# Adding u to the destination rows on GpSimd instead of VectorE, with u in two buffers

## The chip, the cores and the metric

The kernel runs on one core of a Trainium2 chip. The metric is the device time of one execution in microseconds; the time before is the median of three runs. Engines are named as the profile names them: PE is TensorE's matmul side and PEld its weight loads, DVE is VectorE, ACT is ScalarE, POOL is GpSimd, SP is SyncE, which here only issues DMAs.

## The reference, cut to what matters

The network is four graph layers over 100,000 nodes with 64 features and 50,000 edges sorted by destination. The change touches the end of the first layer, graph attention with four heads: per edge the source row `hs` and the destination's own row `hd` are each weighted by head, added, projected by `gatw`, summed over the edges of one destination, biased and passed through a leaky relu of slope 0.01. The result is added to the node's row x.

```python
    alpha = ex / denom[d2]
    o = jax.ops.segment_sum(xh[s2] * alpha[:, :, None], d2, num_segments=n)
    o = jnp.mean(o, axis=1) + gat_b
    return _leaky(o, NEG_ACT)
...
    x = x + _L0_gnn_ref(h, edge_index, edge_weight, ...)
```

## The kernel before

The edges are cut into 49 groups of 1024 (128 partitions by S = 8 slots, C = 64 features each). The program is a row of stages with a barrier between them; every engine has its own loop over the groups in each stage. The stage in question is `attention_sums`. `ring_loop` gives each engine, in step s, the work of group s minus a lag, in the order of the numbers that the generators yield; four steps are unrolled in a hardware loop. Engines meet only at semaphores, and each engine works strictly in its written order.

In step s the engines do the following.

- DVE: copies a count of group s-1 (L1902, short "copy"), multiplies the source rows by the weights into `at_wide` for s-1 (L1903, "mul"), scans the projected sums of s-3 (L1308, "scan"), forms u = max(slant, row) of s-4 from PSUM and `at_slant` (L1922, "u"), adds u to the destination rows `at_xd` into `at_x1` (L1928, "x"; the profile calls the tile `at_x`), and adds the own rows to the last six slots of `at_wide` of s-1 (L1908, "add").
- POOL: multiplies the own rows of slots 0 to 3 of group s (L1880, "own"), then, once DVE's mul of s is done, adds the first two slots into `at_wide` (L1883, "joined").
- PE: transposes the weights of s (L1938), transposes `at_wide` of s-2 (L1950), transposes the biased sums of s-4 back (L412), and multiplies by `gatw` for s-2 (L1959), which waits for the scan of the group before.
- ACT: evacuates the weights (L1977) and the transposed rows (L1993, "pf"), computes `at_slant` (L2007, "slant"), the biased sums (L2000), and 16 small products of the own rows (L1984).
- SP: issues the loads of the groups, the load of `at_xd` four groups ahead, and the store of `at_x1`; the last two wait for the semaphore `x1_done`.

What a step counts from in this text is the start of its scan, called S.

Of the kernel before, what the change touches and what calls it, by code (L numbers as in the profile page):

```python
# [22 lines left out]
ALU = mybir.AluOpType  # L23
# [8 lines left out]
P = 128  # L32
C = 64
S = 8
# [3 lines left out]
GROUPS = -(-EDGES // G_ROWS)  # L38
# [19 lines left out]
RING = 4  # L58
# [24 lines left out]
def take_turns(stages):  # L83

    due = [(0, k, gen) for k, gen in enumerate(stages)]
    while due:
        due.sort(key=lambda x: x[:2])
        t, k, gen = due.pop(0)
        nxt = next(gen, None)
        if nxt is not None:  # L90
            assert nxt >= t, (nxt, t)
            due.append((nxt, k, gen))


def ring_loop(eng, n, *lags, lead=0, ring=RING):

    k_max = max(len(lags) + 1, lead)
    assert n > k_max + ring

    def step(group_of):  # L100
        started = []
        for k, stages in enumerate(lags):
            at = group_of(k)
            if at is not None:
                started += [s for s in (f(*at) for f in stages) if s is not None]
        take_turns(started)

    def fixed(s):
        def at(k):
            g = s - k  # L110
            return (g // ring, g % ring, g) if 0 <= g < n else None
        step(at)

    for s in range(k_max):
        fixed(s)
    turns = (n - k_max) // ring
    with eng.Fori(0, turns) as i:  # L117
        for q in range(ring):
            def at(k):
                off = k_max + q - k  # L120
                return i + off // ring, off % ring, i * ring + off
            step(at)
    for s in range(k_max + ring * turns, n + len(lags) - 1):
        fixed(s)


def hold(eng, sem, value):


    if not (isinstance(value, int) and value < 1):  # L130
        eng.wait_ge(sem, value)  # L131
        eng.sem_inc(HELD[0], 1)  # L132


def after(eng, sem, value):

    if not (isinstance(value, int) and value < 1):
        eng.wait_ge(sem, value)
# [6 lines left out]
def half_turns(i, r):  # L145

    return i * 2 + r // 2
# [295 lines left out]
def as_rows(x):  # L443
    return x.rearrange("p (s c) -> p s c", c=C)
# [14 lines left out]
def build(nc, A, out):  # L459
    ctx = ExitStack()  # L460
    with ctx:
# [101 lines left out]
        with ExitStack() as kept:  # L563
# [7 lines left out]
            phase(attention_sources, W, D, bank, M)  # L571
            phase(attention_weights, W, D, bank, M)
        phase(attention_sums, W, D, bank)
        phase(gated_messages, W, D, bank)
        phase(relu_messages, W, D, bank, out)
# [1251 lines left out]
def attention_sums(nc, A, sem, W, D, bank):  # L1827

    ctx = ExitStack()
    with ctx:  # L1830
        t = lambda n, sh, dt=F32: ctx.enter_context(nc.sbuf_tensor(n, sh, dt))
        col = W.col
        hs, hd = (t("at_" + n, [P, 2, S, C]) for n in ("hs", "hd"))
        xd, x1 = t("at_xd", [P, RING, S, C + 1]), t("at_x1", [P, 2, S, C])
# [3 lines left out]
        pf = t("at_pf", [P, 2, 2, HALF])  # L1838
        sums = t("at_sums", [C, 2, G_ROWS])
        biased = t("at_biased", [C, 2, G_ROWS])  # L1840
        slant, u = (t("at_" + n, [P, S, C]) for n in ("slant", "u"))
        names = ("al_t", "al_done", "wide_step", "joined", "own_done", "own_rest", "wide_t", "pf_done", "mm", "carry", "biased_done", "u_done",
                 "back", "slanted", "x1_done")
        m = {n: sem("at_" + n) for n in names}
        inn, st = ([sem(f"at_{n}{k}") for k in (0, 1)] for n in ("in", "st"))
        x_in = [sem(f"at_x_in{r}") for r in range(RING)]
        with nc.Block() as block:
            @block.sync
            def _(sp):
                for k in (0, 1):  # L1850
                    sp.sem_inc(st[k], 16)

                def load(i, r, g):
                    hold(sp, m["wide_step"], g * 2 + 1)
                    sp.wait_ge(m["own_done"], g + 1)
                    sp.wait_ge(m["own_rest"], g + 1)
                    for b, d in ((hs, D.hs), (hd, D.hd)):
                        sp.dma_start(b[:, r % 2], group_rows(d)[g]).then_inc(inn[r % 2], 16)
                    sp.dma_start(alpha[:, r % 2], group_cols(D.alpha)[g]).then_inc(inn[r % 2], 16)

                def load_x(i, r, g):
                    sp.wait_ge(m["x1_done"], g + 1)
                    sp.dma_start(xd[:, r], group_rows(D.xd)[g]).then_inc(x_in[r], 16)

                def store(i, r, g):
                    sp.wait_ge(m["x1_done"], g + RING + 1)
                    sp.dma_start(group_rows(D.x1d)[g], x1[:, r % 2]).then_inc(st[r % 2], 16)
                ring_loop(sp, GROUPS, [load], [], [load_x], [], [], [], [store])
                for k in (0, 1):
                    sp.wait_ge(st[k], ODD_EVEN[k] + 16)  # L1870

            @block.gpsimd
            def _(pool):
                def own_rows(i, r, g):
                    hold(pool, inn[r % 2], half_turns(i, r) * 48 + 48)
                    hold(pool, m["al_done"], g + 1)
                    hold(pool, m["wide_step"], g * 2 + 2)
                    rows = hd[:, r % 2, 0:S // 2].unsqueeze(2).to_broadcast([P, S // 2, HEADS, C])
                    by = al[:, r % 2, 0:S // 2, HEADS:2 * HEADS].unsqueeze(3).to_broadcast([P, S // 2, HEADS, C])
                    nc.gpsimd.tensor_tensor(own[:, r % 2, 0:S // 2], rows, by, ALU.mult).then_inc(m["own_done"], 1)  # L1880
                    hold(pool, m["own_done"], g + 3)
                    hold(pool, m["wide_step"], g * 2 + 5)
                    nc.gpsimd.tensor_tensor(wide[:, r % 2, 0:JOINED], wide[:, r % 2, 0:JOINED], own[:, r % 2, 0:JOINED], ALU.add  # L1883
                                            ).then_inc(m["joined"], 1)
                ring_loop(pool, GROUPS, [own_rows])

            @block.vector
            def _(dve):
                dve.sem_inc(m["wide_step"], 4)
                dve.sem_inc(m["own_done"], 2)  # L1890
                dve.sem_inc(m["own_rest"], 2)
                dve.sem_inc(m["x1_done"], RING)
                nc.vector.memset(sums[:, 1, G_ROWS - 1:G_ROWS], 0.0).then_inc(m["carry"], 1)

                def a(i, r, g):
                    yield 1
                    dve.wait_ge(inn[r % 2], half_turns(i, r) * 48 + 48)
                    dve.wait_ge(m["al_done"], g + 1)
                    after(dve, m["wide_t"], g * 2 - 2)
                    by = hs[:, r % 2].unsqueeze(2).to_broadcast([P, S, HEADS, C])  # L1900
                    wt = al[:, r % 2, :, 0:HEADS].unsqueeze(3).to_broadcast([P, S, HEADS, C])
                    nc.vector.tensor_copy(W.countE[:, bass.ds(g, 1)], al[:, r % 2, :, 2 * HEADS].unsqueeze(1))  # L1902
                    nc.vector.tensor_tensor(wide[:, r % 2], by, wt, ALU.mult).then_inc(m["wide_step"], 1)  # L1903
                    yield 4
                    dve.wait_ge(m["wide_step"], g * 2 + 5)
                    dve.wait_ge(m["own_done"], g + 3)
                    dve.wait_ge(m["own_rest"], g + 3)
                    nc.vector.tensor_tensor(wide[:, r % 2, JOINED:S], wide[:, r % 2, JOINED:S], own[:, r % 2, JOINED:S], ALU.add  # L1908
                                            ).then_inc(m["wide_step"], 1)

                def scan(i, r, g):
                    yield 2
                    dve.wait_ge(m["mm"], g + 1)
                    dve.wait_ge(m["carry"], g + 1)
                    after(dve, m["biased_done"], g - 1)
                    run_sums(nc, W, g, r % 2, bank(4, 2)[0:C], sums, m)

                def x(i, r, g):
                    yield 3
                    dve.wait_ge(m["slanted"], g + 1)  # L1920
                    after(dve, m["x1_done"], g + RING)
                    nc.vector.scalar_tensor_tensor(out=u[:], in0=as_rows(bank(1)), scalar=0.0, in1=slant[:], op0=ALU.add,  # L1922
                                                   op1=ALU.max).then_inc(m["u_done"], 1)
                    yield 3
                    dve.wait_ge(x_in[r], i * 16 + 16)
                    dve.wait_ge(st[r % 2], half_turns(i, r) * 16 + 16)
                    dve.wait_ge(m["u_done"], g + 1)
                    nc.vector.tensor_tensor(x1[:, r % 2], xd[:, r, :, 0:C], u[:], ALU.add).then_inc(m["x1_done"], 1)  # L1928
                ring_loop(dve, GROUPS, [], [a], [], [scan], [x])

            @block.tensor
            def _(pe):
# [658 lines left out]
```

## Time and profile before

| what | value |
|---|---|
| median of three runs | 5640.13 us (5633.73 to 5650.66) |
| profiled execution, its span from the first instruction to the last | 5641.0 us |
| busy in the span: PE, DVE, ACT, POOL | 66%, 74%, 42%, 67% |
| mean granted PE clock | 0.777 |
| the stage `attention_sums` | 2963 us to 3371 us |

The page gives the profiled execution by its span alone. The shares of the whole span are averages over stages with different limits. The stage of the change is 408 us of the 5641, so it is read by itself.

### The profile page before, as it was taken

What the parts mean: (1) busy time and instruction counts of PE and PEld (TensorE: products, weight loads), DVE (VectorE), ACT (ScalarE), POOL (GpSimd) and SP (SyncE); (2) the same over time, 40 slices, a digit from 0 to 9 for tenths busy, and PEclk for the clock granted to TensorE, in tenths of its full rate; (3) what the DMA queues carried; (4) which work ended last, traced back from release to release, by engine and by line L of the source; (5) the groups of instructions that cost most, each with busy time, mean ns of one, the idle gap of its engine ahead of it and who ended that gap; (6) DMA issues with size and microseconds to landing.
All of it is one profiled execution on the core that took longest, in us unless ns stands there. A gap on an engine that the chain in (4) does not pass through costs nothing. (4 is left out here: it accounts for less than half of the span.)

```text
span 5641.0 us, 69641 instructions
## 1 busy us (share of the span) xinstructions
PE 3732.6 (66%) x15267; PEld 1851.4 (33%) x15267; DVE 4168.8 (74%) x6266; ACT 2361.1 (42%) x4957; POOL 3788.1 (67%) x3734
## 2 busy tenths in 40 slices
PE   8997788847776999677727876777555546552110
PEld 3443555533332333244414442333222212221000
DVE  8876789957774555788868988999655559996442
ACT  0000678833331222466618973343222247772221
POOL 7776766767775777577724337666377767774777
PEclk9998899977876555788869998899766568885555
DMA  5533987744442222455524433333244423332221
GB/s 59 77 53 56 153 203 226 234 136 107 107 106 55 61 63 61 141 182 171 181 64 129 137 117 76 82 83 82 79 130 131 131 69 76 76 73 65 68 72 51
DMA packets 538641, 595.34 MB, mean 106 GB/s; under 512 B 300576, under 2 KB 315046, under 8 KB 536923
## 3 DMA queue, kind: packets, MB, share of 16 engines
q1 hardware_dynamic: 319004, 473.91, 28.7%
q0 software_dynamic: 115712, 91.82, 9.1%
q10 hardware_dynamic: 103840, 28.71, 4.2%
q14 instruction: 59, 0.48, 0.0%
q8 instruction: 26, 0.43, 0.0%
HBM read 354.69 MB, written 303.31 MB: 117 GB/s over the span
## 5 line engine op out<-in xcount | busy, mean ns | idle before, releaser
L1135 POOL DMA_INDIRECT l_got<-d_x,l_near x1176 | 1157.6, 984 | 557.5 <-issue 354.6
L1135 POOL DMA_INDIRECT p_got<-d_h,p_near x392 | 440.2, 1123 | 155.8 <-issue 118.9
L848 PE MATMUL ps<-hot_lo,hot_w 128*128 128x512 bf16 x2352 | 510.0, 380 | 13.4 <-DVE hot_lo L785 13.4
L1135 POOL DMA_INDIRECT p_got<-d_sums,p_near x392 | 401.4, 1024 | 151.7 <-issue 149.3
L2457 POOL DMA_INDIRECT out<-fi_res,fi_near x392 | 381.0, 972 | 181.1 <-issue 118.2
L726 POOL DMA_INDIRECT d_pos<-place,near x392 | 400.2, 1021 | 125.2 <-issue 119.1
L1135 POOL DMA_INDIRECT p_got<-d_ext,p_near x392 | 382.2, 975 | 132.4 <-issue 117.1
L1143 POOL DMA_INDIRECT ln_xd<-d_xt,idsE x304 | 286.9, 944 | 136.8 <-issue 96.9
L2131 PE MATMUL ps<-l_hid,w2n 128*64 128x512 f32 x392 | 234.8, 756 | 162.2 <-DVE l_sums L1308 155.7
L412 PE MATMUL ps<-ident,fi_sums 64*128 64x64 f32 x392 | 53.1, 314 | 424.8 <-DVE fi_sums L1308 424.8
L848 PEld LDWEIGHTS ps<-hot_lo,hot_w 128*128 128x128 bf16 x2352 | 230.6, 98 | 293.2 <-issue 17.3
L782 DVE SCALAR_TENSOR_TENSOR hot_w<-iota_hi,hiS,vals 128x384 bf16<-128x384 bf16 x392 | 241.1, 615 | 80.8 <-PE ps L848 78.2
L1308 DVE TENSOR_TENSOR_SCAN p_sums<-same,p_sums,ps 65x1024 f32<-65x1024 f32 (+1 forms) x98 | 229.6, 2343 | 93.5 <-PE ps L1407 89.5
L405 PE MATMUL ps<-ident,l_hn 128*128 128x128 f32 x588 | 112.2, 323 | 221.4 <-DVE l_hn L2236 196.9
L419 PE MATMUL ps<-l_df,l3ab 128*64 128x512 f32 x196 | 164.8, 995 | 127.5 <-DVE l_neg L2357 127.5
L1308 DVE TENSOR_TENSOR_SCAN l_sums<-same,l_sums,ps 64x1024 f32<-64x1024 f32 (+1 forms) x98 | 228.7, 2334 | 0.4
L1883 POOL TENSOR_TENSOR at_wide<-at_wide,at_own 128x512 f32<-128x512 f32 x49 | 70.3, 1434 | 215.9 <-DVE at_wide L1903 214.7
L1959 PE MATMUL ps<-at_pf,gatw 128*64 128x512 f32 x392 | 178.3, 598 | 54.1 <-DVE at_sums L1308 53.5
L2524 DVE TENSOR_TENSOR fi_res<-fi_xd,ps 128x512 f32<-128x512 f32 x49 | 33.5, 684 | 241.7 <-POOLq L2464 241.7
L419 PE MATMUL ps<-l_hf,l2w 128*64 128x512 f32 x196 | 176.8, 1058 | 46.5 <-ACT l_hf L2280 46.5
L863 ACT ACTIVATE near<-finE 128x8 int32 (+1 forms) x49 | 10.2, 208 | 467.3 <-DMA d_pos<-place,near 467.3
L2545 ACT ACTIVATE ps<-fi_hh,fi_sc 64x1024 f32<-64x1024 f32 x49 | 59.0, 1205 | 337.0 <-DMA fi_hh<-d_hh 333.1
(391 smaller groups left out, 10871.3 us busy)
## 6 DMA issues: line engine op xcount, KB each, us to landing
l_xd<-d_x SPq DMA_DIRECT2D x147, 256.0 KB
d_ext<-ln_ext SPq DMA_DIRECT2D x98, 264.0 KB
d_xt<-in_x_wide ACTq DMA_DIRECT2D x49, 520.0 KB
ln_x<-in_x SPq DMA_DIRECT2D x98, 256.0 KB
d_h<-ln_hb SPq DMA_DIRECT2D x98, 256.0 KB, 2.9
d_x<-ln_x SPq DMA_DIRECT2D x98, 256.0 KB
lb_x<-d_x SPq DMA_DIRECT2D x49, 512.0 KB
d_x<-lb_x SPq DMA_DIRECT2D x49, 512.0 KB
```

Of the source, the lines that this page charges most:

```text
L405: last = nc.tensor.transpose(out[:, P * n:P * n + P], flat[:, P * n:P * n + P], W.ident[:])
L419: last = nc.tensor.matmul(out[:, HALF * h:HALF * h + HALF], weights[:, h], paired, start=True, stop=True)
L726: nc.gpsimd.indirect_dma_start(out=D.pos, out_offset=bass.IndirectOffsetOnAxis(ap=near[:, r, q:q + 1], axis=0), in_=at[:, r, q:q + 1], in_ ...
L782: nc.vector.scalar_tensor_tensor(out=hot_w[:, r], in0=wide(iota_hi[:], PARTS), scalar=hs[:, one], in1=vt.unsqueeze(2).to_broadcast([P, PAR ...
L848: last = nc.tensor.matmul(bank(h), hot_w[:, r, k], hot_lo[:, r, 512 * h:512 * h + 512], start=False, stop=False)
L1135: nc.gpsimd.indirect_dma_start(out=out[:, q], out_offset=None, in_=source, in_offset=bass.IndirectOffsetOnAxis(ap=ids[:, q:q + 1], axis=0) ...
L1143: nc.gpsimd.indirect_dma_start(out=out[:, q], out_offset=None, in_=source, in_offset=bass.IndirectOffsetOnAxis(ap=ids[:, g, q:q + 1], axis ...
L1308: return nc.vector.tensor_tensor_scan(sums[:, par], same, messages, sums[:, 1 - par, G_ROWS - 1:G_ROWS], ALU.mult, ALU.add).then_inc(m["ca ...
L1883: nc.gpsimd.tensor_tensor(wide[:, r % 2, 0:JOINED], wide[:, r % 2, 0:JOINED], own[:, r % 2, 0:JOINED], ALU.add).then_inc(m["joined"], 1)
L1959: last = nc.tensor.matmul(bank(4, 2)[0:C, HALF * h:HALF * h + HALF], W.gatw[:, q], pf[:, h, q], start=q == 0, stop=q == 1)
L2131: last = nc.tensor.matmul(msg[:, part], W.w2n[:], hid[k][:, part], start=k == 0, stop=k == 1)
L2457: nc.gpsimd.indirect_dma_start(out=out, out_offset=bass.IndirectOffsetOnAxis(ap=near[:, r, q:q + 1], axis=0), in_=res[:, r, q], in_offset= ...
```

## The change

x is taken from DVE's list and put into POOL's, at the same lag of four groups. In POOL's code the lag decides only the group; within a step POOL runs own, joined, x in that order. `at_u` becomes two buffers, so u of a group may be written while x of the group before is still to come: DVE's u waits for the x of two groups before (`g + RING - 1`) instead of one. POOL's x waits for `at_xd`, for the store that used the same half of `at_x1`, and for u; `hold` is a wait followed by a semaphore increment.

```diff
-        slant, u = (t("at_" + n, [P, S, C]) for n in ("slant", "u"))
+        slant, u = t("at_slant", [P, S, C]), t("at_u", [P, 2, S, C])
...
-                ring_loop(pool, GROUPS, [own_rows])
+
+                def x(i, r, g):
+                    hold(pool, x_in[r], i * 16 + 16)
+                    hold(pool, st[r % 2], half_turns(i, r) * 16 + 16)
+                    hold(pool, m["u_done"], g + 1)
+                    nc.gpsimd.tensor_tensor(x1[:, r % 2], xd[:, r, :, 0:C], u[:, r % 2], ALU.add).then_inc(m["x1_done"], 1)
+                ring_loop(pool, GROUPS, [own_rows], [], [], [], [x])
...
-                def x(i, r, g):
+                def rows(i, r, g):
                     yield 3
                     dve.wait_ge(m["slanted"], g + 1)
-                    after(dve, m["x1_done"], g + RING)
-                    nc.vector.scalar_tensor_tensor(out=u[:], in0=as_rows(bank(1)), scalar=0.0, in1=slant[:], op0=ALU.add,
+                    after(dve, m["x1_done"], g + RING - 1)
+                    nc.vector.scalar_tensor_tensor(out=u[:, r % 2], in0=as_rows(bank(1)), scalar=0.0, in1=slant[:], op0=ALU.add,
                                                    op1=ALU.max).then_inc(m["u_done"], 1)
-                    yield 3
-                    dve.wait_ge(x_in[r], i * 16 + 16)
-                    dve.wait_ge(st[r % 2], half_turns(i, r) * 16 + 16)
-                    dve.wait_ge(m["u_done"], g + 1)
-                    nc.vector.tensor_tensor(x1[:, r % 2], xd[:, r, :, 0:C], u[:], ALU.add).then_inc(m["x1_done"], 1)
-                ring_loop(dve, GROUPS, [], [a], [], [scan], [x])
+                ring_loop(dve, GROUPS, [], [a], [], [scan], [rows])
```

On DVE, one step in the loop of the stage stood like this before (a scan is listed as SCALAR_TENSOR_TENSOR; ISA and REGISTER_ALU rows are waits and their register arithmetic).

```order
L1308 SCALAR_TENSOR_TENSOR at_sums<-same,at_sums,ps 64x1024
L1922 SCALAR_TENSOR_TENSOR at_u<-ps,at_slant 128x512
L1928 TENSOR_TENSOR at_x<-at_xd,at_u 128x512
L1905 REGISTER_ALU
L1906 REGISTER_ALU
L1908 TENSOR_TENSOR at_wide<-at_wide,at_own 128x1536
```

In the changed kernel the same step reads as follows; x is gone, and the add stands right behind u.

```order
L1308 SCALAR_TENSOR_TENSOR at_sums<-same,at_sums,ps 64x1024
L1928 SCALAR_TENSOR_TENSOR at_u<-ps,at_slant 128x512
L1911 REGISTER_ALU
L1912 REGISTER_ALU
L1914 TENSOR_TENSOR at_wide<-at_wide,at_own 128x1536
```

On POOL, this is a piece of the same loop before.

```order
L1880 TENSOR_TENSOR at_own<-at_hd,at_al 128x1024
L131 REGISTER_ALU x2
L1883 TENSOR_TENSOR at_wide<-at_wide,at_own 128x512
L131 REGISTER_ALU
L131 ISA
L1880 TENSOR_TENSOR at_own<-at_hd,at_al 128x1024
```

In the changed kernel x stands between joined and the next group's own.

```order
L1880 TENSOR_TENSOR at_own<-at_hd,at_al 128x1024
L131 REGISTER_ALU x2
L1883 TENSOR_TENSOR at_wide<-at_wide,at_own 128x512
L131 ISA x2
L131 REGISTER_ALU
L1890 TENSOR_TENSOR at_x<-at_xd,at_u 128x512
L131 REGISTER_ALU
L131 ISA
L1880 TENSOR_TENSOR at_own<-at_hd,at_al 128x1024
```

So x moved past every DVE instruction of a step and behind POOL's joined, and own of the next group now starts behind it. The order on PE, ACT and SP is the same as before.

## Rows read from the trace of the kernel before

**Rows 1.** Window of the steady part: busy us of each engine, PE clock.

```profile
core 0: us, PE busy (x) PEld busy (x) DVE busy (x) ACT busy (x) POOL busy (x), PEclk, DMA share, GB/s
...
3003.50:3351.60 348.10, 296.29 (x1754) 170.49 (x1752) 334.15 (x266) 326.34 (x924) 138.00 (x88) 1.00 0.47 138
```

**Rows 2.** Timeline of DVE, steady: start us, us, work, idle before and its releaser.

```profile
3153.85 2.33 DVE L1308 TENSOR_TENSOR_SCAN at_sums<-same,at_sums,ps 64x1024 f32<-64x1024 f32 x1
3156.28 0.69 DVE L1922 SCALAR_TENSOR_TENSOR at_u<-ps,at_slant 128x512 f32<-128x512 f32 x1
3157.08 0.72 DVE L1928 TENSOR_TENSOR at_x<-at_xd,at_u 128x512 f32<-128x512 f32 x1
3157.72 1.75 DVE L1908 TENSOR_TENSOR at_wide<-at_wide,at_own 128x1536 f32<-128x1536 f32 x1
3159.39 0.16 DVE L1902 COPY countE<-at_al 128x8 f32 x1
3159.47 2.28 DVE L1903 TENSOR_TENSOR at_wide<-at_hs,at_al 128x2048 f32<-128x2048 f32 x1
3161.67 2.33 DVE L1308 TENSOR_TENSOR_SCAN at_sums<-same,at_sums,ps 64x1024 f32<-64x1024 f32 x1
3164.30 0.69 DVE L1922 SCALAR_TENSOR_TENSOR at_u<-ps,at_slant 128x512 f32<-128x512 f32 x1 [0.30 <-ACT at_slant L2007]
```

**Rows 3.** Timeline of POOL, the same stretch.

```profile
3154.11 1.27 POOL L1883 TENSOR_TENSOR at_wide<-at_wide,at_own 128x512 f32<-128x512 f32 x1 [4.88 <-DVE at_wide L1903]
3155.35 1.90 POOL L1880 TENSOR_TENSOR at_own<-at_hd,at_al 128x1024 f32<-128x1024 f32 x1
```

**Rows 4.** Timeline of PE, the same stretch.

```profile
3156.57 3.62 PE L1959 MATMUL ps<-at_pf,gatw 128*64 128x512 f32 x8 [1.27 <-DVE at_sums L1308]
...
3160.71 1.97 PE L1950 MATMUL ps<-ident,at_wide 128*128 128x128 f32 x16
```

**Rows 5.** Timeline of ACT, the same stretch.

```profile
3163.67 0.60 ACT L2007 ACTIVATE at_slant<-ps 128x512 f32<-128x512 f32 x1
```

**Rows 6.** Timeline of DVE, the stage's head.

```profile
2973.12 1.76 DVE L1908 TENSOR_TENSOR at_wide<-at_wide,at_own 128x1536 f32<-128x1536 f32 x1 [1.86 <-POOL at_own L1880]
2974.79 1.23 DVE L1902 COPY countE<-at_al 128x8 f32<-128x8 f32 x1
2975.94 2.28 DVE L1903 TENSOR_TENSOR at_wide<-at_hs,at_al 128x2048 f32<-128x2048 f32 x1
```

**Rows 7.** Timeline of POOL, the stage's head.

```profile
2973.30 2.70 POOL L1883 TENSOR_TENSOR at_wide<-at_wide,at_own 128x512 f32<-128x512 f32 x1 [0.27 <-POOL at_own L1880]
2975.96 4.03 POOL L1880 TENSOR_TENSOR at_own<-at_hd,at_al 128x1024 f32<-128x1024 f32 x1
```

**Rows 8.** Timeline of DVE, the first steady step.

```profile
3003.55 2.33 DVE L1308 TENSOR_TENSOR_SCAN at_sums<-same,at_sums,ps 64x1024 f32<-64x1024 uint8 x1
...
3006.59 0.89 DVE L1928 TENSOR_TENSOR at_x<-at_xd,at_u 128x512 f32<-128x512 f32 x1
```

**Rows 9.** Timeline of POOL, the same step.

```profile
3005.03 1.90 POOL L1880 TENSOR_TENSOR at_own<-at_hd,at_al 128x1024 f32<-128x1024 f32 x1
```

**Rows 10.** Timeline of DVE, the last steady step's scan.

```profile
3351.58 2.33 DVE L1308 TENSOR_TENSOR_SCAN at_sums<-same,at_sums,ps 64x1024 f32<-64x1024 uint8 x1
```

**Rows 11.** Tile at_x on DVE: duration min/median/max in ns, first and last start.

```profile
L1928 DVE TENSOR_TENSOR at_x<-at_xd,at_u x49: 692/693/1173, 2998.5 to 3370.3; 128x512 f32<-128x512 f32 x49
```

**Rows 12.** Timeline of DVE, later in the head.

```profile
2986.40 2.34 DVE L1308 TENSOR_TENSOR_SCAN at_sums<-same,at_sums,ps 64x1024 f32<-64x1024 uint8 x1 [1.21 <-PE ps L1959]
2988.66 1.72 DVE L1908 TENSOR_TENSOR at_wide<-at_wide,at_own 128x1536 f32<-128x1536 f32 x1
...
2990.39 2.28 DVE L1903 TENSOR_TENSOR at_wide<-at_hs,at_al 128x2048 f32<-128x2048 f32 x1
```

**Rows 13.** Timeline of POOL, the same stretch as rows 12.

```profile
2987.29 6.50 POOL L1883 TENSOR_TENSOR at_wide<-at_wide,at_own 128x512 f32<-128x512 f32 x1 [0.34 <-POOL at_own L1880]
```

**Rows 14.** Window of the next stage, columns as in rows 1.

```profile
3500.00:3600.00 100.00, 74.40 (x287) 34.90 (x288) 96.88 (x171) 37.97 (x74) 69.92 (x68) 0.90 0.32 83
```

## The prediction

> **What bounds the kernel now.** I read the windows first, to find out which engine is full in the stage of the change. In the steady part, 348 us long, DVE is busy 96% of the time, ACT 94%, PE 85%, POOL 40%, and PE has its full granted clock (1.00, so 2.4 GHz) [rows 1]. The first scan of it starts at 3003.55 [rows 8], the last at 3351.58 [rows 10], 44 steps later: 7.91 us a step. These 44 steps are what the change can act on; the head of the stage (40 us) and its tail (19 us) are fills and drains.
>
> Then the timelines of one step. On DVE the starts follow each other by: scan to u 2.43 us, u to x 0.80, x to add 0.64, add to copy 1.67, copy to mul 0.08, mul to scan 2.20 [rows 2]. The sum is 7.82 us. Every second step or so u starts some tenths late behind ACT's slant (0.30 us idle at 3164.30 [rows 2]), which makes the mean 7.91. So DVE is the bound, but a second loop is nearly as long: from the end of a scan (3156.18) PE multiplies (3.62 us), then transposes the weights and `at_wide` [rows 4], ACT evacuates and forms slant, which ends at 3164.27 [rows 5], 8.09 us after the scan's end. The u that waits for it leads to the scan after next. Two steps along this loop are 8.09 + 0.03 + 0.80 + 0.64 + 1.67 + 0.08 + 2.20 + 2.33 = 15.84, that is 7.92 a step. Both loops contain x.
>
> The third thing to see is POOL. joined starts 0.26 us after the scan's start, own follows 1.24 us later and takes 1.90, so POOL is done at S+3.40 and then idles until the next mul is done, 4.88 us at joined's row [rows 3]. By busy share it has much room. But look at when it works: only while DVE runs scan and u.
>
> **DVE and POOL get in each other's way.** This is the row reading on which the forecast rests. In the head, own started when mul had just started and took 4.03 us instead of 1.90: it ends at 2979.99, which is 1.77 us after the mul's end at 2978.22 [rows 6, 7]. joined, started inside an add, took 2.70 instead of 1.27 and ended 1.12 after the add's end [rows 6, 7]. The copy behind that add took 1.23 us instead of 0.16 and ended with joined [rows 6, 7]. And x itself took 0.89 us when own was still running, against a median of 0.69 [rows 11]: own ended at 3006.93, x at 3007.48, so x really began 0.14 us before own's end [rows 8, 9]. In the steady step its 0.72 fits the same rule (own ends at 3157.25). Scan and u, which read one operand from PSUM, run beside POOL at full speed, and so does POOL: 2.33 and 0.69, 1.27 and 1.90 [rows 2, 3]. So in this trace a DVE instruction with both operands in SBUF (mul, add, x) and a POOL instruction never overlap: one waits to the end of the other, less 0.14 us of start-up.
>
> The Trainium skill says the same in "SBUF — State Buffer", section Who interferes with whom: DVE instructions with two SBUF inputs and GpSimd instructions that read SBUF share one port pair, and whoever issues first holds it for the whole instruction. The trace agrees where own took 4.03 us beside a mul; by the page's first-come order the step would be the 8.45 us worked out below, and there is one place in the trace where that order did not hold (rival B).
>
> **The change, part by part.** (1) x leaves DVE: u to add becomes 0.65 in place of 0.80 + 0.64 (the 0.80 holds a semaphore wait on u, the 0.64 is what an instruction of this size takes with none). DVE's own work is then 7.82 - 0.80 = 7.02 a step.
>
> (2) x on POOL. The trace has no x there; the nearest row is joined, the same 128x512 f32 addition, 1.27 us, followed by the next instruction after 1.24 [rows 3]. Lower bound: DVE's 0.69. Upper: 1.90, own with twice the elements. I take 1.27. x's three holds (each a wait and an increment) are processed while joined runs, and all are met: u was finished a step earlier, `at_xd` four groups ahead. The store two groups back has about two steps, some 16 us, against one and a half before, when x never waited for it.
>
> (3) Where x lands. joined S+0.26, x S+1.50, own S+2.74 to S+4.64. DVE has u at S+2.43 and wants the add, with both operands in SBUF, at S+3.08. own has started 0.34 us before that, so the add waits until 4.64 - 0.14 = S+4.50. From there add, copy and mul take 1.67 + 0.08 + 2.20, and the next scan starts at S+8.45. Before, own ended at S+3.40, just as x wanted to start at S+3.23: POOL's 3.14 us filled exactly the 3 us in which DVE leaves it alone. The change puts 1.24 us more into a window that was full and takes only 0.80 from DVE.
>
> (4) Does anything hide this? Queued behind x on POOL is own, for whose result the add of the next step waits, one step later: no wait. PE starts transposing `at_wide` at S+6.86 (3160.71 [rows 4]); the late add ends at 4.50 + 1.75 = S+6.25, in time. slant ends 2.33 + 8.09 = S+10.42, at a step of 8.45 that is 1.97 into the next, ahead of u at 2.43. So neither PE nor ACT adds to it nor covers it; the scan waits for DVE alone. SP's load of `at_xd` and the store wait for x, now later by nearly a step; both had more than that.
>
> (5) The second buffer of u costs nothing; with one, u would have waited for the x before, done at S+2.77, past u's S+2.43.
>
> (6) Ends of the stage: in the head the longest x (1.17 us [rows 11], half of it waiting for own) no longer stands before an add that would wait for the same own: about -0.6. The last x of the stage runs 1.27 for 0.69 on POOL: +0.6. They cancel.
>
> Sum: 44 x (8.45 - 7.91) = +23.8 us. On the profiled execution's 5641.0 that is 5664.8; this execution is 0.9 above the median of the runs, so I forecast 5664 for the median, 0.4% slower.
>
> **Rivals.** (A) *No collision that matters, and faster.* If the add took the port before own and own lost nothing by it, or POOL's additions read from elsewhere, the step would be the longer of 7.02 and the PE and ACT loop without x: (15.84 - 0.80) / 2 = 7.52. 44 x 0.39 = -17, 5623. It decides where own no longer stands between u and add. Against it stand four rows of collisions and no row of an overlap. 5%.
>
> (B) *Milder: POOL's work is packed tighter.* In one place joined was issued at 2987.29 during a scan with an add queued behind, and did not run: it ended at 2993.79, 1.12 after the end of the mul that began at 2990.39, having let add, copy and mul pass [rows 12, 13]. So a queued DVE instruction can be served first. If this happens behind u, own slips past the mul and POOL's three run in one piece from there: 1.12 for the one already waiting, then 1.24 and 1.90, with small overlaps 4.18 after S, giving a step of 4.18 + 3.95 = 8.13, 44 x 0.22 = +10, 5650. This is the least that exclusive use allows. But a group that is late on POOL makes PE wait for joined, and then PE's loop lengthens the step again toward 8.5. 15%, of which most is within 0.3%.
>
> (C) *Worse: own slips in behind the add*, as joined did in the head [rows 6, 7]. Then the add runs from S+3.08 to 4.83, own to 6.60, and the copy starts at 6.46, mul at 6.54, the scan at 8.74: 44 x 0.83 = +36, 5676. 10%.
>
> (D) *The clock.* PE's busy share falls from 85% to 6.73 / 8.45 = 80%. In the next stage PE is 74% busy and has a clock of 0.90 [rows 14], that is, part of it at 1.2 GHz. Were PE's work from its matmuls to the first half of the `at_wide` transposes (4.14 us between their starts, and 1.0 [rows 4]) to take twice as long, the loop without x would be (15.04 + 5.1) / 2 = 10.1 a step. If a tenth of the steady part fell to it: 4.4 x 1.7 = +7 on top, 5671. 10%.
>
> **How the numbers follow.** The forecast has 60%; its own range is 5658 to 5669, from x at 1.1 us (a step of 8.30) to 1.4 (8.58), with 44 steps each. Adding (B), (C) and (D) gives 5645 to 5678, which leaves out (A), and the rest of the surprises. What a measurement here tells from no change is about 0.3%, 17 us. Slower by more: nearly all of the forecast, (C) and (D), 0.77. Within: most of (B) and the low edge, 0.18. Faster: 0.05.
>
> **What would show it.** Right: in the changed profile the steady scans start 8.4 to 8.5 us apart; the add has a mean near 3.2 us (it waits inside its duration, as x's 0.89 did) in place of 1.75; x on POOL lasts 1.27 and starts 1.5 behind the scan; own starts at S+2.74 undisturbed at 1.90; slant no longer holds up u; DVE still looks 95% busy, by waiting. (B) would show as own or x of 5 to 6 us and adds at 1.75. (C) as a copy of 1.8 us. (A) as idle time of DVE before u behind slant and a step of 7.5. Wrong altogether would be a step below 7.9 or a stage that grew anywhere but in its steady part.

## The result, and the profile after

The changed kernel takes 5663.9 us (median of 6 runs, 5654.75 to 5666.86), beside 5639.69 us for the kernel before (6 runs, 5633.73 to 5650.66). The ratio is 1.0038, 95% interval 1.0026 to 1.0049: 15 to 28 us slower. The profiled execution of it took 5664.0 us, with a span of 5661.4; the span of the one before is 5641.0, so by spans it is +20.4. One run of the kernel before, on the second chip of the experiments, took 8855.53 us and is left out of the ratios.

The page's busy line, to be read against the one of before in the table above:

```profile
PE 3736.0 (66%) x15267; PEld 1848.1 (33%) x15267; DVE 4173.5 (74%) x6217; ACT 2361.5 (42%) x4957; POOL 3861.7 (68%) x3783
```

The window of the 44 steady steps, columns as in rows 1:

```profile
2999.40:3368.40 369.00, 319.63 (x1742) 174.82 (x1741) 341.25 (x221) 326.28 (x923) 198.94 (x132) 0.93 0.41 129
```

It is 369.1 us from scan to scan (2999.39 to 3368.46), in place of 348.0 [rows 8, 10]: +21.0, or 8.39 us a step against 7.91. DVE lost 45 instructions and 30 us of real work to POOL, and yet is busy 7 us longer, 92% of the window. The head of the stage, from its first mul to this scan, became 0.6 us shorter (34.6 to 34.0), its tail 0.8 longer (19.4 to 20.2). So the stage holds +21.2. The rest of the span moved by -3.6 us ahead of the stage and +2.7 behind it, where nothing was changed.

One steady step on DVE:

```profile
3117.93 2.33 DVE L1308 TENSOR_TENSOR_SCAN at_sums<-same,at_sums,ps 64x1024 f32<-64x1024 f32 x1
3120.19 0.65 DVE L1928 SCALAR_TENSOR_TENSOR at_u<-ps,at_slant 128x512 f32<-128x512 f32 x1
3120.77 3.31 DVE L1914 TENSOR_TENSOR at_wide<-at_wide,at_own 128x1536 f32<-128x1536 f32 x1
3124.00 0.16 DVE L1908 COPY countE<-at_al 128x8 f32 x1
3124.08 2.28 DVE L1909 TENSOR_TENSOR at_wide<-at_hs,at_al 128x2048 f32<-128x2048 f32 x1
3126.28 2.33 DVE L1308 TENSOR_TENSOR_SCAN at_sums<-same,at_sums,ps 64x1024 f32<-64x1024 f32 x1
```

And the same step on POOL:

```profile
3118.19 1.26 POOL L1883 TENSOR_TENSOR at_wide<-at_wide,at_own 128x512 f32<-128x512 f32 x1 [4.08 <-DVE at_wide L1909]
3119.42 1.17 POOL L1890 TENSOR_TENSOR at_x<-at_xd,at_u 128x512 f32<-128x512 f32 x1
3120.56 1.90 POOL L1880 TENSOR_TENSOR at_own<-at_hd,at_al 128x1024 f32<-128x1024 f32 x1
```

The add is issued at S+2.84 and lasts 3.31 us in place of 1.75 [rows 2]. No idle time is shown: the 1.56 us of waiting lie inside its duration. own runs from S+2.63 to S+4.53, that is to 3122.46, and the add ends where an add of 1.75 us would that began 0.14 us before: 3122.46 - 0.14 + 1.75 = 3124.07, against 3124.08 shown. The step is 8.35 us.

The tiles, duration min/median/max in ns:

```profile
L1890 POOL TENSOR_TENSOR at_x<-at_xd,at_u x49: 1164/1175/6422, 3000.9 to 3387.5; 128x512 f32<-128x512 f32 x49
L1914 DVE TENSOR_TENSOR at_wide<-at_wide,at_own x49: 1737/2844/3307, 2969.6 to 3372.2; 128x1536 f32<-128x1536 f32 x49
```

x lasts 1.18 on POOL, not 1.27. The add has a median of 2.84 (a mean of 2.62 over the 44 steps), and sometimes 1.74: not every step looks like the one above. In some steps a block of PE's matmuls takes longer, as the first of these two, while the transposes of `at_wide` behind it keep their 1.97 us:

```profile
3154.05 5.31 PE L1960 MATMUL ps<-at_pf,gatw 128*64 128x512 f32 x8 [1.54 <-DVE at_sums L1308]
...
3162.42 3.65 PE L1960 MATMUL ps<-at_pf,gatw 128*64 128x512 f32 x8
```

The mean granted clock of the window is 0.93, so parts of it are at 1.2 GHz. The slant that hangs on the slow matmuls is late for the scan after next, in 12 of the 40 regular steps described below, as here on DVE:

```profile
3159.67 2.33 DVE L1308 TENSOR_TENSOR_SCAN at_sums<-same,at_sums,ps 64x1024 f32<-64x1024 f32 x1
3163.47 0.69 DVE L1928 SCALAR_TENSOR_TENSOR at_u<-ps,at_slant 128x512 f32<-128x512 f32 x1 [1.47 <-ACT at_slant L2008]
3164.08 1.75 DVE L1914 TENSOR_TENSOR at_wide<-at_wide,at_own 128x1536 f32<-128x1536 f32 x1
...
3168.03 2.33 DVE L1308 TENSOR_TENSOR_SCAN at_sums<-same,at_sums,ps 64x1024 f32<-64x1024 f32 x1
```

and on POOL:

```profile
3162.30 1.90 POOL L1880 TENSOR_TENSOR at_own<-at_hd,at_al 128x1024 f32<-128x1024 f32 x1
```

Read by its releaser alone, this step is held up by slant. But own ends at 3164.20 and the add would have waited until 3164.06 in any case; it is issued at 3164.08. The step is 8.36 us, as the one of 8.35 without any lateness: two waits lie side by side, 0.02 us apart, and only the longer is paid. Of the 44 steps, 40 are 8.33 to 8.39 us long. The first four are 6.78, 10.07, 9.47 and 8.73; the first two on DVE:

```profile
3002.23 1.74 DVE L1914 TENSOR_TENSOR at_wide<-at_wide,at_own 128x1536 f32<-128x1536 f32 x1
...
3003.97 2.27 DVE L1909 TENSOR_TENSOR at_wide<-at_hs,at_al 128x2048 f32<-128x2048 f32 x1
...
3009.75 0.69 DVE L1928 SCALAR_TENSOR_TENSOR at_u<-ps,at_slant 128x512 f32<-128x512 f32 x1 [1.25 <-ACT at_slant L2008]
3010.35 1.97 DVE L1914 TENSOR_TENSOR at_wide<-at_wide,at_own 128x1536 f32<-128x1536 f32 x1
3012.25 1.87 DVE L1908 COPY countE<-at_al 128x8 f32 x1
```

and on POOL:

```profile
3002.01 6.01 POOL L1880 TENSOR_TENSOR at_own<-at_hd,at_al 128x1024 f32<-128x1024 f32 x1
...
3010.68 3.42 POOL L1880 TENSOR_TENSOR at_own<-at_hd,at_al 128x1024 f32<-128x1024 f32 x1
...
3017.72 6.42 POOL L1890 TENSOR_TENSOR at_x<-at_xd,at_u 128x512 f32<-128x512 f32 x1
```

Here own, issued 0.22 us ahead of the add, let add, copy and mul pass and ended 1.78 us after the mul's end: the order of rival (B), and a step of 6.78. In the next one slant was late, the add went first, own slipped in behind it and the copy waited: rival (C), 10.07. The pair costs 16.85, that is 8.43 a step. In the third step it is x that is held, 6.42 us in place of 1.18, until 1.05 us after the end of the mul at 3023.09. But what sets this step is PE:

```profile
3018.96 6.61 PE L1960 MATMUL ps<-at_pf,gatw 128*64 128x512 f32 x8 [3.23 <-DVE at_sums L1308]
```

The block takes 6.61 us in place of 3.62, at a granted clock of 0.54; the next scan waits 2.61 us for it, and the step is 9.47. Here, once, the lower clock does cost: the third and fourth steps together are 1.5 us longer than two of 8.35, the first pair only 0.15. Together the four are 1.6 us longer than four of 8.35.

### The profile page after: what moved, and what is told of

It is laid out like the page before. It is cut to its first block and busy times, and to the rows that moved or that the text cites. A ratio compares the mean times of both kernels' runs of the same rounds, so it can differ in the third digit from the quotient of the medians.

```text
span 5661.4 us, 69751 instructions
## 1 busy us (share of the span) xinstructions
PE 3736.0 (66%) x15267; PEld 1848.1 (33%) x15267; DVE 4173.5 (74%) x6217; ACT 2361.5 (42%) x4957; POOL 3861.7 (68%) x3783
## 5 line engine op out<-in xcount | busy, mean ns | idle before, releaser
L1960 PE MATMUL ps<-at_pf,gatw 128*64 128x512 f32 x392 | 203.8, 669 | 50.5 <-DVE at_sums L1308 49.2
L1438 ACT ACTIVATE p_slant<-ps 64x1024 f32<-64x1024 f32 x49 | 49.8, 1017 | 350.7 <-DVE ps L1390 350.7
```

Source lines behind the costliest of these rows:

```text
L1960: last = nc.tensor.matmul(bank(4, 2)[0:C, HALF * h:HALF * h + HALF], W.gatw[:, q], pf[:, h, q], start=q == 0, stop=q == 1)
```

## The experiments

Three groups, each on one chip with its own runs of the kernel before (medians 5646.40, 5641.87 and 5660.58 us; medians of one kernel differ between these chips by up to 19 us, as much as most of the changes cost, so ratios are compared). The first four rows are one group, the next four the second, the last four the third. "Step" is the mean of 44 steps of the profiled execution, from the third scan on.

| | median us (runs) | ratio to before, 95% | step us |
|---|---|---|---|
| without x | 5628.07 (7) | 0.9966 (0.9955 to 0.9977) | 7.59 |
| spare add, full window | 5697.36 (4) | 1.0089 (1.0072 to 1.0106) | 9.05 |
| spare add behind own | 5698.29 (4) | 1.0096 (1.0079 to 1.0113) | 9.02 |
| memset behind own | 5644.91 (10) | 1.0005 (0.9996 to 1.0015) | 8.06 |
| the change again | 5658.81 (5) | 1.0034 (1.0019 to 1.0048) | 8.35 |
| the change, one u | 5660.93 (6) | 1.0034 (1.0022 to 1.0047) | 8.35 |
| the change, short own | 5619.24 (5) | 0.9963 (0.9949 to 0.9977) | 7.50 |
| swap | 5639.04 (11) | 0.9996 (0.9986 to 1.0005) | 8.55 |
| the change, PE filled | 5685.08 (9) | 1.0034 (1.0024 to 1.0045) | 8.39 |
| swap, PE filled | 5655.40 (10) | 0.9988 (0.9978 to 0.9998) | 7.79 |
| swap, one more execution | 5663.58 (1) | | 7.79 |
| the change, x behind own | 5669.80 (10) | 1.0014 (1.0005 to 1.0024) | 8.21 |

### What x costs on DVE

```diff
 (before)
-nc.vector.scalar_tensor_tensor(out=u[:], in0=as_rows(bank(1)), ...)
-nc.vector.tensor_tensor(x1[:, r % 2], xd[:, r, :, 0:C], u[:], ALU.add)
+nc.vector.scalar_tensor_tensor(out=x1[:, r % 2], in0=as_rows(bank(1)), ...)
```

Not in these lines: whoever waited for x waits for u here.

> The kernel before with x left out: DVE's u goes straight into the buffer that is stored, so the destination rows are not added. POOL has its two old instructions. Theory (port collision with own sets the changed kernel's step): with x gone and nothing put on POOL, own ends at S+3.40 and lets the add begin at S+3.26, so DVE alone would need 7.2 us a step and the PE and ACT loop sets about 7.5: some 17 us under the kernel before (ratio 0.997). Rival (the step of before was set by something other than DVE's chain through x, and moving x off DVE can never pay): no difference, and then the 24 us of the change have another origin than POOL's extra instruction.

19 us faster by the ratio, with steps of 7.22 and 8.0 in turn, a mean of 7.59 where 7.5 was expected. In those where slant is early, the add meets own. On DVE:

```profile
3141.83 1.94 DVE L1908 TENSOR_TENSOR at_wide<-at_wide,at_own 128x1536 f32<-128x1536 f32 x1
```

on POOL:

```profile
3140.25 1.91 POOL L1880 TENSOR_TENSOR at_own<-at_hd,at_al 128x1024 f32<-128x1024 f32 x1
```

This step's scan starts at 3138.76. Even with nothing put on POOL, own's end at S+3.40 holds the add for 0.19 us. So taking x away altogether is worth 19 us, and putting it on POOL turns that into a loss of about the same size.

### What an addition costs on POOL, by its place

```diff
 (before; own_rows on POOL)
 nc.gpsimd.tensor_tensor(wide[:, r % 2, 0:JOINED], ..., own[:, r % 2, 0:JOINED], ALU.add)   # joined
+nc.gpsimd.tensor_tensor(spare[:, 0:HALF], own[:, r % 2, 0:JOINED]..., own[:, r % 2, JOINED:2 * JOINED]..., ALU.add)
```

> The kernel before, x still on DVE, with one more POOL addition of 128x512 f32 (into a spare buffer that nobody reads) between joined and own. DVE's work is the same as before. Theory: own ends at about S+4.5, x begins at S+4.39, and add, copy and mul follow: a step of 4.39 + 0.64 + 3.95 = 8.98, 47 us over the kernel before (ratio 1.008). Rival (the changed kernel is slower for the path of x, its waits or its store, not for the port): POOL is idle for 4.9 us a step, so one more instruction there costs nothing, ratio 1.000.

DVE and then POOL in a step that starts at 3173.64:

```profile
3176.68 2.12 DVE L1932 TENSOR_TENSOR at_x<-at_xd,at_u 128x512 f32<-128x512 f32 x1
3178.72 1.74 DVE L1912 TENSOR_TENSOR at_wide<-at_wide,at_own 128x1536 f32<-128x1536 f32 x1
```

```profile
3175.13 1.26 POOL L1886 TENSOR_TENSOR at_spare<-at_own 128x512 f32<-128x512 f32 x1
3176.35 1.91 POOL L1881 TENSOR_TENSOR at_own<-at_hd,at_al 128x1024 f32<-128x1024 f32 x1
```

x waits 1.43 us for own inside its 2.12. Nothing was taken from DVE here, POOL stays idle 4.68 us of each step, and the kernel is 51 us slower, where 47 was expected. The second one puts the same addition into POOL's idle time:

```diff
 nc.gpsimd.tensor_tensor(own[:, r % 2, 0:S // 2], rows, by, ALU.mult)
 hold(pool, m["own_done"], g + 3)
+nc.gpsimd.tensor_tensor(spare[:, 0:HALF], own[:, r % 2, 0:JOINED]..., own[:, r % 2, JOINED:2 * JOINED]..., ALU.add)
 hold(pool, m["wide_step"], g * 2 + 5)
```

> The same spare addition, but between own and joined, where POOL idles before it waits for the mul, beside DVE's x, add and mul. Theory (a DVE instruction with two SBUF operands and a POOL instruction that reads SBUF exclude each other wherever they meet): each addition costs DVE about its 1.0 to 1.2 us in some gap, a step of 8.8 to 9.0, 40 to 47 us over before. Rival (only the place behind joined matters, because it delays own): no difference.

DVE, then POOL:

```profile
3160.43 2.82 DVE L1912 TENSOR_TENSOR at_wide<-at_wide,at_own 128x1536 f32<-128x1536 f32 x1
```

```profile
3160.13 1.50 POOL L1883 TENSOR_TENSOR at_spare<-at_own 128x512 f32<-128x512 f32 x1 [0.18 <-POOL at_own L1881]
```

The same price, 52 us, above the 40 to 47 expected. POOL's idle time is not free time: the addition is issued while x runs, waits for it, and then holds the add for its 1.1 us. That is so in 28 of the 44 steps; in the others, where u is late, the addition starts ahead of x and x waits inside its own duration. The last puts an instruction there that only writes:

```diff
 nc.gpsimd.tensor_tensor(own[:, r % 2, 0:S // 2], rows, by, ALU.mult)
 hold(pool, m["own_done"], g + 3)
+nc.gpsimd.memset(spare[:], 0.0)
```

> As the run with a spare addition between own and joined, but with a POOL memset of 128x1024 f32 in its place, an instruction of about 1 us that only writes. Theory (it is the reading of SBUF that collides with DVE's two-operand instructions): no difference from before, within 0.3%. Rival (any POOL instruction in that place collides, because the writes do, too): 35 to 45 us slower, as with the addition.

DVE, then POOL:

```profile
3142.22 0.69 DVE L1930 TENSOR_TENSOR at_x<-at_xd,at_u 128x512 f32<-128x512 f32 x1
3142.83 1.75 DVE L1910 TENSOR_TENSOR at_wide<-at_wide,at_own 128x1536 f32<-128x1536 f32 x1
```

```profile
3142.49 0.95 POOL L1883 MEMSET at_spare<- 128x1024 f32 x1 [0.15 <-POOL at_own L1881]
```

No difference that can be measured in the times. The memset runs across the end of x and the start of the add, and all three keep their full speed. What DVE and POOL exclude each other from is a thing that reading additions use and a memset doesn't; it isn't that POOL is busy.

The Trainium skill, "SBUF — State Buffer", section Who interferes with whom, names that thing: a DVE instruction with two SBUF inputs contends with a GpSimd instruction that reads SBUF, not with one that only writes. These three runs agree: 51 and 52 us for the additions, and for the memset a ratio whose interval ends at 8 us.

The profiled execution of this kernel is less even than the one of before. Its first eight steady steps take 8.04 to 9.34 us, at a granted clock of 0.90 and with every second block of matmuls at 5.2 to 5.3 us; the other 36 take 7.91 on the mean at 1.00, as before. In the eight the memset keeps its 0.95 and the add its 1.75, and x takes 0.90 at most, as in [rows 8]. So they aren't a collision; whether the memset has a part in the lower clock isn't shown.

### The second buffer of u

The change itself was run again beside the next three, on the same chip.

> The changed kernel itself, so that the runs of this call have it on the same chip: 1.0038 of before, 20 to 25 us.

It came at 1.0034, 17 us above the median beside it, a little under the 20 to 25 expected. All 44 steps are 8.33 to 8.40 us, with none of the irregular ones, and the clock is 0.93 again.

```diff
 (after)
-after(dve, m["x1_done"], g + RING - 1)
-nc.vector.scalar_tensor_tensor(out=u[:, r % 2], ...)
+after(dve, m["x1_done"], g + RING)
+nc.vector.scalar_tensor_tensor(out=u[:], ...)
```

> The changed kernel with one buffer for u, so that DVE's u waits for the x of the group before. x on POOL ends at S+2.67 and u would start about S+2.77 instead of S+2.26, the add would want to start at S+3.4, but it waits for own until S+4.39 anyway. Theory (own's end sets the step): same as the changed kernel, a step of 8.35. Rival (u's place sets it): 0.5 us a step more, 22 us over the changed kernel.

DVE in a step that starts at 3141.96:

```profile
3144.74 0.69 DVE L1928 SCALAR_TENSOR_TENSOR at_u<-ps,at_slant 128x512 f32<-128x512 f32 x1 [0.44 <-POOL at_x L1890]
3145.34 2.77 DVE L1914 TENSOR_TENSOR at_wide<-at_wide,at_own 128x1536 f32<-128x1536 f32 x1
```

u now waits for x, to S+2.78, and the add waits as much less for own. The ratio is that of the change run beside it, 1.0034. The buffer is worth nothing as long as own comes behind x.

### A shorter own

```diff
 (after; own_rows)
-nc.gpsimd.tensor_tensor(own[:, r % 2, 0:S // 2], rows, by, ALU.mult)
+nc.gpsimd.tensor_tensor(own[:, r % 2, 0:JOINED], rows, by, ALU.mult)    # 2 of the 4 slots
```

Not in these lines: memsets ahead of the loop set the other two slots to zero.

> The changed kernel with POOL's own cut to half its elements (two slots instead of four; the other two slots' own rows are zero, so their share is left out of the sums). own then takes about 1.27 us instead of 1.90 and ends 0.63 earlier. Theory (own's end sets the step one for one): a step of about 7.7, 28 us under the changed kernel, 5 under the kernel before. Rival (PE's stretches at half clock, which delay slant to S+3.8 in every second step of the changed kernel, set those steps as well): only half of the steps get shorter, a mean of about 8.0, 14 us under the changed kernel.

DVE, then POOL, in a step that starts at 3138.67:

```profile
3141.62 0.69 DVE L1931 SCALAR_TENSOR_TENSOR at_u<-ps,at_slant 128x512 f32<-128x512 f32 x1 [0.62 <-ACT at_slant L2011]
3142.23 1.75 DVE L1917 TENSOR_TENSOR at_wide<-at_wide,at_own 128x1536 f32<-128x1536 f32 x1
```

```profile
3141.31 1.04 POOL L1880 TENSOR_TENSOR at_own<-at_hd,at_al 128x512 f32<-128x512 f32 x1
```

40 us faster than the change run beside it, and 21 faster than before by the ratio. I had taken this own at 1.27 and expected 7.7; it is 1.04, ends at S+3.68, and the add, issued at S+3.56 behind a late slant, no longer waits for it. What is left is the loop through PE, ACT and slant, at 7.50 us a step. The forecast had worked that loop out as 7.52 for rival (A). So the change would gain, if POOL's reading work fitted into the time from scan to add.

### Giving POOL less to read: the swap

joined goes to DVE (the add covers all eight slots, 2048 elements, 2.28 us), and x comes a group later, behind own:

```diff
 (after)
-nc.gpsimd.tensor_tensor(wide[:, r % 2, 0:JOINED], wide[:, r % 2, 0:JOINED], own[:, r % 2, 0:JOINED], ALU.add)
-ring_loop(pool, GROUPS, [own_rows], [], [], [], [x])
+ring_loop(pool, GROUPS, [own_rows], [], [], [], [], [x])
-hold(pe, m["joined"], g + 1)
-nc.vector.tensor_tensor(wide[:, r % 2, JOINED:S], wide[:, r % 2, JOINED:S], own[:, r % 2, JOINED:S], ALU.add)
+nc.vector.tensor_tensor(wide[:, r % 2], wide[:, r % 2], own[:, r % 2], ALU.add)
```

> x on POOL, one group later, right behind own, and in exchange joined is taken off POOL: DVE adds the own rows of all eight slots (2.28 us instead of 1.75). POOL's two instructions, 1.90 and 1.18, then fit in the 3 us in which DVE scans and forms u. Theory: DVE 7.41 - 7.55 a step, the PE and ACT loop (15.05 + 0.53) / 2 = 7.79, so 5 us under the kernel before (ratio 0.999), hardly to be measured. Rival (any x on POOL costs, wherever it stands): as slow as the changed kernel.

No measurable difference to before in the median, but a spread from 5630.69 to 5673.38, and the profiled execution was the slowest of them. So one more execution of the same kernel was profiled, on another chip.

> The swapped kernel once more, for one look at an execution. The median of its other runs, 5639, asks for a mean step of 7.8 to 7.9; if this execution is such a one, its matmuls are all 3.6 us and own and x keep the places that they had.

The window of the first profiled execution, then that of the second:

```profile
3003.00:3340.00 337.00, 298.24 (x1569) 160.17 (x1567) 295.75 (x196) 291.82 (x828) 118.88 (x78) 0.90 0.42 127
```

```profile
3003.00:3340.00 337.00, 293.44 (x1746) 169.62 (x1744) 320.84 (x216) 320.57 (x912) 135.88 (x85) 1.00 0.46 138
```

The same code, and a tenth less work done in the same 337 us: the clock is 0.90 in one and 1.00 in the other, the steps alternate between 8.0 to 8.3 and 9.0 to 9.1 in the one, between about 7.6 and 7.95 in the other. In the slow one every second block of matmuls reads like this one:

```profile
3140.14 5.26 PE L1955 MATMUL ps<-at_pf,gatw 128*64 128x512 f32 x8 [2.03 <-DVE at_sums L1308]
```

PE had idled 2.03 us before it. The loop through PE and ACT was worked out as 7.79 a step; 1.64 us more in one block of two makes it 8.6, and 8.55 was measured. The same pattern stands in the profile of the change at 0.93, so the next pair asks what it is worth there.

### Taking the clock away: PE filled

```diff
 (after, and the swap; in d on PE, behind transpose_back)
+hold(pe, m["pf_done"], g * 2 + 5)
+for n in range(6):
+    nc.tensor.transpose(bank(2)[:, 0:P], W.ident[:], W.ident[:])
```

> The changed kernel with six more 128x128 transposes of the identity on PE in each step, into a PSUM bank that is free there, in the gap in which PE waits for the scan (0.8 us of otherwise idle time). If they keep PE at 2.4 GHz, the long matmul rows of 5.3 us and the late slant go. Theory (own's end alone sets the step): 8.35 us a step all the same, 1.0034 to 1.0038 of before. Rival (the stretches at 1.2 GHz carry part of the 24 us): a step below 8.3 and some 5 to 15 us under the changed kernel.

The window of the change with PE filled:

```profile
3024.80:3393.80 369.00, 333.41 (x2020) 199.30 (x2019) 358.02 (x221) 330.88 (x924) 226.07 (x132) 1.00 0.43 129
```

The clock is 1.00, no block of matmuls takes more than 3.65, and the regular steps are 8.35 all the same; the ratio is 1.0034 again. So the clock's fall is no part of what the regular step costs: the late slant hides behind own. Pairs of 6.78 and 10.13 are no work of the clock either: here six of them come early on (own at 6.02, copy at 1.87) and a seventh of 8.00 and 9.05, which makes the mean 8.39.

> The swapped kernel (x on POOL, joined on DVE) with the same six transposes. The profiled execution of the swapped kernel had matmuls of 5.1 to 5.3 us in every second step and a mean step of 8.55 us, 30 us more than its other runs. Theory (that was the PE clock at half in a repeating pattern): with PE kept busy the pattern does not start, steps are 7.8 us and all runs lie near 5636. Rival (the long steps came from own or x on POOL): the profile again shows steps of 8 to 9 us.

DVE, then POOL, in the swap with PE filled:

```profile
3145.09 2.33 DVE L1308 TENSOR_TENSOR_SCAN at_sums<-same,at_sums,ps 64x1024 f32<-64x1024 f32 x1
3147.87 0.69 DVE L1924 SCALAR_TENSOR_TENSOR at_u<-ps,at_slant 128x512 f32<-128x512 f32 x1 [0.45 <-ACT at_slant L2006]
3148.48 2.28 DVE L1910 TENSOR_TENSOR at_wide<-at_wide,at_own 128x2048 f32<-128x2048 f32 x1
```

```profile
3145.28 1.91 POOL L1880 TENSOR_TENSOR at_own<-at_hd,at_al 128x1024 f32<-128x1024 f32 x1 [4.61 <-DVE at_wide L1905]
3147.15 1.19 POOL L1886 TENSOR_TENSOR at_x<-at_xd,at_u 128x512 f32<-128x512 f32 x1
```

POOL is done at S+3.25 and nobody waits for it: 7.79 a step as worked out, and 7 us less than before (the interval says 1 to 12). On this chip its runs lie at 5648 to 5661, not at 5636, as the kernel before is slower here, too. That is the lowest ratio here of a kernel that does all the work, by an amount at the edge of what can be told.

### x behind own

```diff
 (after; order on POOL in a step: own, x a group later, joined)
+yield 0    # ahead of own
+yield 2    # ahead of joined
+yield 1    # ahead of x
-ring_loop(pool, GROUPS, [own_rows], [], [], [], [x])
+ring_loop(pool, GROUPS, [own_rows], [], [], [], [], [x])
```

> The changed kernel with x one group later and behind own (POOL: own, x, joined, instead of own, joined, x). In DVE's free window then run joined and own, which end at S+3.40; the add begins at S+3.26, and x has to fit in behind the add or waits until the next scan. Theory (own, joined and x must all find a place in which DVE reads at most one operand from SBUF): no order of the three saves the collision, it comes to 3.26 + 1.67 + 1.03 + 0.08 + 2.20 = 8.24 a step, 15 us over before. Rival (only an x ahead of own costs): 7.2 by DVE, 7.5 by the PE and ACT loop, 17 us under before.

DVE, then POOL, in a step that starts at 3164.08:

```profile
3166.94 2.15 DVE L1917 TENSOR_TENSOR at_wide<-at_wide,at_own 128x1536 f32<-128x1536 f32 x1
3169.02 1.15 DVE L1911 COPY countE<-at_al 128x8 f32 x1
```

```profile
3165.57 1.91 POOL L1881 TENSOR_TENSOR at_own<-at_hd,at_al 128x1024 f32<-128x1024 f32 x1
3167.43 2.70 POOL L1893 TENSOR_TENSOR at_x<-at_xd,at_u 128x512 f32<-128x512 f32 x1
```

The add waits for own to 3167.34, x waits for the add, the copy for x: the course of rival (C), in 42 of the 44 steps, and 8.20, where 8.24 was expected. The ratio is 1.0014, 8 us over before (3 to 14) where 15 was expected, beside the 1.0034 of the change. So an x behind own costs, too, if less. The copy reads one operand, from SBUF, and it waited for x all the same, 1.15 us in place of 0.16: the rule of the forecast, that instructions with two operands in SBUF wait, is too narrow.

## Why the prediction was right, and where not

**The bound and the collision: right.** That DVE and POOL don't read at the same time is what sets the step. The added addition costs 51 and 52 us in two places while the memset costs nothing that can be measured; cutting own by half gives back 40 us. The sum's place (own from behind x, the add waiting inside its duration, POOL's end less 0.14) is to be read in the 40 regular steps, inside the add's duration where u is early and just covered where u is late.

**The size: one term off.** Step (2) took x at 1.27, the duration of joined; it is 1.18. own therefore starts at S+2.62 and not S+2.74, the add is free at S+4.39 and not S+4.50, and the step is 8.35 and not 8.45. That makes 44 x 8.35 - 348.0 = +19.4 in place of +23.8. The four irregular steps add 1.6, which the sum had not (most of it by the block of 6.61 us), and with its ends the stage comes to +21.2, the whole span to +20.4. That the median still came out at the forecast is partly chance: the two medians lie 24 us apart, the two profiled executions 20, and on another chip the medians of the same two kernels 17. Two slips stand in the sum besides, and neither decides anything: 5641.0 is a span, to which the changed kernel's times add 1.9 to 3.0 us, so it can't be set against the median of times; and an x of 1.1 us gives a step of 8.28, not 8.30.

The signs that were named missed by as little: steps of 8.35 for 8.4 to 8.5, own at S+2.62 for S+2.74, DVE 92% busy for 95%. The mean of the add missed by more, 2.62 for 3.2, because of the late steps below.

The Trainium skill had the better figure for step (2): "GPSIMD Engine Reference", section 3.1 Elementwise — side-by-side cycle accounting, gives 4497 ns for an addition of 2048 elements at about 2.6 cycles each, and reckons with 1.2 GHz. An estimate from it for 512 elements is 1.11 us, and 1.17 with the remainder of 0.06 us; x measured 1.18. Why joined, of the same size, takes 1.27 isn't known.

**"slant no longer holds up u": wrong.** Step (4) put slant at 1.97 into the next step, taking PE's matmuls at 3.62 us. Under the change PE's clock is 0.93 on the mean, and in 12 of the 40 regular steps, behind a block of 5.31, u comes at S+3.80; in the step after it, at S+2.69. The falling clock was rival (D), and its mechanism is there, in more than a tenth of the steps. Its price is not: 0.01 us a step and not 1.7, but for the one block of 6.61 among the first four steps. (D) let all of PE's stretch from the matmuls to the `at_wide` transposes take twice as long, +5.1 us on two steps. In the trace only the block of matmuls is longer, by 1.69, and at most every second one, which makes the loop (15.04 + 1.69) / 2 = 8.37 a step, and own's 8.35 covers that almost to the end. Without own's wait, in the swapped kernel, the same pattern does cost: 8.55 for 7.79. With PE filled it is gone from the change, and the regular steps stay at 8.35.

**Step (5): right.** One buffer of u gives the same time, with u waiting to S+2.78. (The forecast had x done at S+2.77; it is done at S+2.67, and u follows 0.11 later.)

**Step (6): right in the numbers, by luck in the head.** Head -0.6, tail +0.8 for -0.6 and +0.6. In the tail 0.5 us are the longer last x, as named. In the head the first scan comes 0.4 later and the two steps behind it are 1.0 shorter together, which is another course than the single x that was named.

**The rivals.** (A) did not come in any steady step; its loop of 7.52 is real, and is what the kernel with a short own runs at. (B) and (C) each came in the first steps, alternating, at 8.43 a step, and six more times as such a pair with PE filled: the bare 8.13 of (B) was never seen, as its own text says ("lengthens the step again toward 8.5"). As the regular course neither took hold.

**Open.** At 3002.01 own was issued 0.37 us behind u and 0.22 ahead of the add, and was passed over; at 3120.56 it was issued 0.37 behind u and 0.21 ahead of the add, and went first. The x at 3017.72 fits an order of issue even less: DVE ran only the scan and u for 1.36 us from there until the add was issued, 1.18 us would have done for x, and it ended behind the mul. Nothing in these rows tells such cases from the regular ones, and no run was made that would.

## What to carry to other kernels

Before work is moved from DVE to GpSimd, look not at GpSimd's idle share but at what DVE runs in the same microseconds: here only the scan and u, which read PSUM, left room for a GpSimd instruction that reads SBUF, and that room, 3 us a step, was already full. Even the copy, with one operand, waited. A wait of this kind shows no idle time, only a duration that is too long; compare each duration with the shortest of its kind. And where two waits end at the same moment, taking away the one that the trace names gives nothing: find the other first.

## What the runs showed of the hardware that was not expected

- **Who goes first isn't settled by who was issued first.** own on POOL, issued 0.22 us ahead of the add, ended behind add, copy and mul at 6.01 us in the kernel after, and seven times at 6.0 with PE filled. x did so at 6.42 us though it was issued 1.36 us ahead of the add. In the regular steps the one issued first ran first.
- **POOL's durations for one size differ by operands.** 128x512 elements: 1.18 (x), 1.27 (joined), 1.04 (half of own, with broadcast inputs), 1.26 (the spare add).
- **One kernel can run at either clock.** The swapped kernel had steps of 7.79 us with a granted clock of 1.00, and of 8.55 with 0.90, which is partly at 1.2 GHz: a block of matmuls takes 3.65 and 5.26 us in turn, the longer one behind 2.03 us of idle time. Its times spread over 43 us (11 runs). With six spare transposes a step the clock was 1.00 and the spread 13 us (10 runs), but on another chip, where one execution without them had 1.00, too. Of the changed kernel three profiles without the transposes have 0.93 (one of them with one buffer for u) and the one with them 1.00. That the idle time keeps the clock down is a guess from this.
